# A graph kernel's front: three count tables in turn, zeroed in 16 blocks, with the input read early and its products pipelined

## The reference, cut to what matters

```python
deg = jnp.maximum(segment_sum(ones, dst, 2500), 1.0)
norm = deg ** (-0.5)
h = jnp.maximum(_layernorm(x), 0.0)
hw = norm * (h @ weight)                    # w0 in the kernel
agg = segment_sum(hw[src], dst, 2500)
x = x + relu(agg * norm + bias)
h = jnp.maximum(_layernorm(x), 0.0)
# two layers on h: scores of q[tgt] and k[srcidx] along the edges,
# softmax by target, weighted sum of v, Wo, batch norm, feed-forward
```

## Time and profile before

| | us |
|---|---|
| median of 3 runs | 3387.66 |
| lowest and highest | 3385.79, 3404.86 |
| profiled execution, device time | 3393.12 |
| its span | 3391.3 |
| zeros issued, and landed by the first scatter | 4.1, 73.2 |
| first and last scatter | 73.2, 914.4 |
| last projection of the front ends | 974.0 |

### The profile page before, as it was taken

How to read it: one execution, slowest core, us unless ns; L and a number is a source line. 1 busy time by engine, 2 the same in 40 slices (tenths; PEclk the granted TensorE clock), 3 DMA queues, 4 the chain that set the end, 5 groups by cost and what they waited for, 6 DMA issues and landing times. The chain is left out here.

```text
span 3391.3 us, 72342 instructions
## 1 busy us (share of the span) xinstructions
PE 2990.1 (88%) x24802; PEld 2279.6 (67%) x24802; DVE 2267.0 (67%) x6951; ACT 1965.5 (58%) x3918; POOL 2155.7 (64%) x1991
## 2 busy tenths in 40 slices
PE   2368999978869999999999989989999999999985
PEld 2124655645537778887787877757777778888874
DVE  8594334332337888888888853227888888888856
ACT  0123444433337788888787821227787788888834
POOL 1687877778617777777777710007777777777734
PEclk9999999988989999999999989999999999999998
DMA  9666666645579888888888831238898988888852
GB/s 372 102 126 157 125 122 130 114 91 92 99 194 171 168 166 170 170 175 175 162 167 174 156 84 25 52 72 177 166 166 166 174 171 171 168 173 173 162 120 61
DMA packets 1297462, 496.76 MB, mean 146 GB/s; under 512 B 1237240, under 2 KB 1262865, under 8 KB 1291408
## 3 DMA queue, kind: packets, MB, share of 16 engines
q1 hardware_dynamic: 1156197, 460.22, 63.7%
q0 software_dynamic: 133120, 0.80, 4.2%
q10 hardware_dynamic: 7788, 31.21, 2.8%
HBM read 153.55 MB, written 80.48 MB: 69 GB/s over the span
## 5 line engine op out<-in xcount | busy, mean ns | idle before, releaser
L1255 POOL TENSOR_TENSOR staged<-prob,staged 125x500 f16<-125x500 f32 x960 | 1071.3, 1122 | 166.0 <-ACT staged L1249 87.0
L1483 DVE CUSTOM_DVE_ANT_0 prob<-s_ps,mask 125x500 f32<-125x500 f32 x1600 | 1042.3, 673 | 179.5 <-PE s_ps L1333 116.2
L1420 ACT ACTIVATE prob<-prob,neg_max 125x1000 f32<-125x1000 f32 (+1 forms) x960 | 954.7, 994 | 58.9 <-DVE scrap L1489 53.8
L1333 PE MATMUL s_ps<-keys,queries 128*128 128x500 f16 x3200 | 945.7, 377 | 43.7 <-DMA queries<-q_tiles 28.0
L529 POOL DMA_INDIRECT counts<-count,cell x320 | 653.3, 2042 | 256.3 <-issue 98.1
L1361 PE MATMUL o_ps<-values,across 125*128 125x128 f16 x7680 | 586.8, 219 | 63.9 <-DMA across<-staged 63.4
L1361 PEld LDWEIGHTS o_ps<-values,across 125*128 125x128 f16 x7680 | 502.7, 97 | 200.8 <-issue 70.1
L1249 POOL CAST staged<-prob 125x500 f16<-125x500 f32 x640 | 385.5, 602 | 334.4 <-ACT prob L1420 201.6
L1496 DVE TENSOR_TENSOR p_lo<-t_ps,p_hi 125x500 f16<-125x500 f32 x640 | 434.4, 679 | 171.6 <-ACT p_hi L1430 167.2
L1430 ACT CAST p_hi<-t_ps 125x500 f16<-125x500 f32 x640 | 364.0, 569 | 146.3 <-PE t_ps L1344 145.0
L1344 PEld LDWEIGHTS t_ps<-identity,prob 125*125 125x125 f32 x2560 | 378.2, 188 | 92.0 <-ACT prob L1420 4.4
(11 more groups left out here) (162 smaller groups left out, 3684.2 us busy)
## 6 DMA issues: line engine op xcount, KB each, us to landing
mask<-bias_rows SPq DMA_DIRECT2D x200, 218.8 KB
counts<-xt ACTq DMA_DIRECT2D x8, 3054.0 KB, 37.2
keys<-counts SPq DMA_DIRECT2D x40, 546.9 KB
bias_rows<-edge_bias SPq DMA_DIRECT2D x20, 1093.8 KB
queries<-q_tiles SPq DMA_DIRECT2D x80, 250.0 KB, 3.9
pair_row<-pair_flat SPq DMA_DIRECT2D x40, 437.5 KB
across<-staged SPq DMA_TRANSPOSE x960, 3.0
q_tiles<-q_both SPq DMA_DIRECT2D x80, 125.0 KB, 3.0
```

The costliest lines, as they stand in the source:

```text
L1255: engine.tensor_tensor(here[0:P, BPC:2 * BPC, 0:P], prob[u % PROBS][:, k * KC:(k + 1) * KC].rearrange("p (s c) -> p s c", s=BPC), here[0:P ...
L1333: mm = pe.matmul(s_ps[n % SB][:, 0:KC], lhsT=queries_sb[b][:, at:at + 128], rhs=keys[:, h, c * KC:(c + 1) * KC], start=(part == 0), stop=( ...
L1420: act.activation(here, here, ACT.Exp, bias=neg_max[u % 4][:, :], accum_out=sums[u // H % 2][:, u % H, piece:piece + 1]).then_inc(exped, 1)
L1483: dve.tensor_tensor_reduce(out=prob[u % PROBS][:, at], in0=s_ps[n % SB][0:P, 0:KC], in1=bias[b][:, at], scale=1.0, scalar=MASKED, op0=ALU. ...
```

## The change

- **Three tables.** `counts` becomes three separate tables of N x N cells, and group q writes table q % 3, behind group q - 3. `load_parts` issues six DMAs instead of four, and `merge` adds twice per piece. The three tables together are 37.5 MB.
- **Zeros in 16 blocks.** A block is a sixteenth of each of the three tables, in 3 DMAs of 0.78 MB (runs of 3052 bytes). ACT issues block 0; SP issues block k once all before it have landed, behind the load of pair row k + 1, which itself waits for one of three buffers (`ROWS = 3`). POOL begins once the zeros that `tallies` 0 to 3 can reach are there (`zeros_due`, worked out on DVE); from scatter 32 on it wants all of them.
- **x early**, in two parts right behind block 0 on ACT.
- **w0 products pipelined:** ACT turns tile t + 1 and makes h of t + 2 before it scales tile t, and PE turns t + 1 before it multiplies t.
- **Norm behind ten tally blocks:** one-hots, `tallies` 0 to 2, degrees, statistics of x, `tallies` 3 to 9, then `norm`.
- The last group of each tile is found with small PE transposes and two DVE operations on 20 partitions instead of 20 on 125. `merge(0)` stands ahead of the wait for `hw`, and `first_done` behind it.

```diff
-SIDES = 2
-ROW = SIDES * N
-ZCOLS = 12216
-ZDMAS = 8
+SIDES = 3
+ZCOLS = 3052
 ZREP = 2
+ZDMAS = 16
+GATED = 4
+ROWS = 3
...
+        def zero_block(engine, k):
+            for n in range(SIDES):
+                engine.dma_start(counts[n][k * ZCELLS:(k + 1) * ZCELLS, :].rearrange("(p r c) o -> p r (c o)", p=128, r=ZREP),
+                                 zero_rows).then_inc(zeroed, 16)
...
+                def load_pairs(k):
+                    if k >= ROWS:
+                        sp.wait_ge(rows_used, k - ROWS + 1)
...
+                load_pairs(0)
+                load_pairs(1)
+                for k in range(1, ZDMAS):
+                    load_pairs(k + 1)
+                    sp.wait_ge(zeroed, SIDES * 16 * k)
+                    zero_block(sp, k)
...
+                for k in range(ZDMAS + 1, NB):
+                    load_pairs(k)
...
-                pool.wait_ge(zeroed, 16 * ZDMAS)
                 for q in range(NG):
                     n, turn = q % SIDES, q // SIDES
                     if q % PER_ROW == 0:
-                        pool.wait_ge(cells_ready, q // PER_ROW + 1)
+                        k = q // PER_ROW
+                        pool.wait_ge(cells_ready, k + 1)
+                        if k < GATED:
+                            blocks = pool.value_load(zeros_due_i[0:1, k:k + 1], min_val=SIDES * 16, max_val=SIDES * 16 * ZDMAS)
+                            pool.wait_ge(zeroed, blocks)
+                            apart(pool, waits_met)
+                        elif k == GATED:
+                            pool.wait_ge(zeroed, SIDES * 16 * ZDMAS)
                     if turn > 0:
                         pool.wait_ge(group_writes[n], 16 * GC * turn)
                         pool.sem_inc(groups_landed, 1)
...
                 def merge(t):
...
-                    for k in range(NKC):
-                        dve.tensor_tensor(cnt[b][:, piece(k)], parts[b][:, piece(k)], parts[b][:, N + k * KC:N + (k + 1) * KC],
-                                          ALU.add).then_inc(merged, 1)
+                    for k in range(NKC + 1):
+                        if k < NKC:
+                            steps.done(dve.tensor_tensor(cnt[b][:, piece(k)], parts[b][0][:, piece(k)], parts[b][1][:, piece(k)],
+                                                         ALU.add))
+                        if k > 0:
+                            steps.wait(but=1 if k < NKC else 0)
+                            dve.tensor_tensor(cnt[b][:, piece(k - 1)], cnt[b][:, piece(k - 1)], parts[b][2][:, piece(k - 1)],
+                                              ALU.add).then_inc(merged, 1)
...
+                nodes_h(0)
+                nodes_h(1)
+                turned_h(0)
+                act.wait_ge(deg_loaded, 16)
+                act.activation(deg_root[:, :], deg_col[:, :], ACT.Sqrt).then_inc(roots_ready, 1)
+                act.wait_ge(norm_ready, 1)
+                for t in range(NT):
+                    if t + 1 < NT:
+                        turned_h(t + 1)
+                    if t + 2 < NT:
+                        nodes_h(t + 2)
+                    scaled_hw(t)
```

More of the change, by code:

```diff
@@ L151, in sb @@
         return ctx.enter_context(nc.sbuf_tensor(name, shape, dt))
-    counts = dram("counts", [TABLE, 1], U16)
+    counts = [dram(f"counts{n}", [TABLE, 1], U16) for n in range(SIDES)]
     bias_rows = dram("bias_rows", [N, N], F32)
@@ L539, in tallies @@
                 def tallies(k):
-                    dve.wait_ge(rows_loaded[k % 2], BOTH * (k // 2 + 1))
+                    dve.wait_ge(rows_loaded[k % ROWS], BOTH * (k // ROWS + 1))
+                    here = tally[k % 2]
+                    if k < GATED:
+                        steps.done(dve.tensor_reduce(most[:, :], pair_row[k % ROWS][0:1, :], AXX, ALU.max))
                     for c in range(BC):
@@ L547, in tallies @@
                         steps.done(dve.scalar_tensor_tensor(
[L548 to L549 removed]
+                            matches[c % 2][:, :], pair_row[k % ROWS][:, own], pair[:, at:at + 1],
+                            earlier[:, after:after + GE], ALU.is_equal, ALU.mult, accum_out=here[:, c:c + 1]))
                     steps.wait()
@@ L589, in _ @@
-                for k in range(EARLY):
-                    tallies(k)
-                for half in range(HALVES):
-                    for t in range(TH):
-                        steps.done(dve.scalar_tensor_tensor(below[:, t, :], dst_i[:, :], float(P * (half * TH + t + 1)),
-                                                            group_i[:, :], ALU.is_lt, ALU.mult))
-                    steps.wait()
-                    steps.done(dve.tensor_reduce(needed[:, half * TH:(half + 1) * TH], below[:, :, :], AXX, ALU.max))
-                    steps.wait()
@@ L599, in _ @@
-                dve.sem_inc(needed_ready, 1)
-                for k in range(EARLY, AHEAD):
-                    tallies(k)
-                dve.wait_ge(x_loaded, BOTH)
+                dve.sem_inc(needed_ready, 1)
+                onehots(0)
+                onehots(1)
+                tallies(0)
+                for q in range(2, 5):
+                    onehots(q)
+                tallies(1)
+                for q in range(5, QP):
+                    onehots(q)
+                tallies(2)
+                dve.wait_ge(onehots_used, QP)
@@ L703, in _ @@
                 merge(0)
+                dve.wait_ge(hw_ready, NT)
+                dve.sem_inc(first_done, 1)
+                dve.wait_ge(bias0_loaded, 16)
                 for t in range(APART):
```

266 lines of the change are left out of this document (164 added, 102 removed).

## The result

The changed kernel takes 3398.38 us (median of 19 runs, 3390.02 to 3409.07) beside 3387.19 us for the kernel before (19 runs, 3378.20 to 3404.86): a ratio of 1.003, with a 95% interval of 1.0018 to 1.0042. It is 11 us slower, where 21 us less were forecast. The profiled execution took 3392.59 us (span 3390.8). From the start of the front's last projection to the end of the span 2405 to 2421 us pass in the 13 profiled executions of this study, with the same code. That spread of 16 us is wider than what the front lost, so the front is read from the traces, and the whole from medians and ratios.

A forecast was written before the change was run, and what follows sets the result against it. Scatters were taken to set when PE starts tile 16, and so the front's end. Tile 16 at 774 instead of 800.8 gave -26.8 us, the last tiles +5.7: -21, from the median 3387.7 to 3367, range 3343 to 3416.

The forecast's parts named there:

- Z: The moment at which all zeros have landed: 73 us in the kernel before, forecast at 180.
- Z, before block 5: DVE's one-hots, first tally blocks and statistics of x, until zero block 5 goes out: 82 us.
- one-hots start at about 10 us: Start of DVE's chain to block 5: the first one-hots at about 10 us.
- Z, from block 5 on: Eleven remaining zero blocks at 8.7 us each, 6.2 for zeros and 2.5 for the gap: Z = 180.
- Rival (1): Zeros are slow, short runs costing per packet as x's do (214 GB/s): Z = 236, time 3423; chance 0.12.
- POOL after Z: Scatters 32 to 274 at 2.35 us, 10 us of landing waits: scatter 274 at Z + 579, tile 16 at Z + 594.
- Rival (3): The third table frees no landing waits, as loads and stores fill the DMA engines: tile 16 at 822, time 3415; chance 0.13.
- DVE and PE after Z: Remaining tallies, merge(0), then PE's tiles: tile 0 about Z + 99, tile 16 at Z + 585.
- The w0 products: PE's products without round trips: 4.35 us a tile instead of 6.50, ending at 200, worth nothing at the end.
- The last tiles: Tile 17 is 3.3 us late, tiles 18 and 19 pay 1.2 each: 5.7 us lost in all.
- The sum: Tile 16 at 774 instead of 800.8 (-26.8), plus 5.7 for the last tiles: -21 us, so 3367.
- point of decision, Z = 201: Up to Z = 201, a zero block of 10.6 us, the change gains; beyond it, slow zeros decide.

The follow-up runs named there:

- e11: The changed kernel with zero blocks 6 to 15 issued one behind the other, no pair row between them and no landing wait: ratio 1.0051, 3399.5 us.
- e3: The changed kernel with two tables instead of three: ratio 1.0035, 3396.1 us.
- e10: The changed kernel with zeros streamed, the early merge, each zero block ahead of the pair row, and two tables: ratio 0.9964, 3369.9 us.
- e4: The changed kernel with the w0 products written one tile behind the other again: ratio 1.003, 3392.5 us.
- e1: The changed kernel with zero blocks 5 to 15 not waiting for the landing of the block before: ratio 0.9987, 3382.3 us.
- e7: The changed kernel with the edits of e1 and e6 together: ratio 0.9948, 3361.6 us.
- e6: The changed kernel with the next tile's load ahead of k and v stores and its merge ahead of this tile's low parts: ratio 0.9974, 3373.3 us.
- e5: The changed kernel with all zeros issued by ACT at the start, x behind them, and POOL waiting for all: ratio 1.0059, 3404.6 us.
- e2: The changed kernel with the third table loaded but not added in tiles 17 to 19: ratio 0.9994, 3380.4 us.

## Why the prediction was wrong

**Z, before block 5: 89 instead of 82.** The step "one-hots start at about 10 us" failed: the load of `src_i` lands at 14.9, ten operations follow, and the first one-hot starts at 17.84 (9.34 before).

```profile
14.90 0.49 DVE L644 SCALAR_TENSOR_TENSOR pair<-dst_i,src_i 125x320 f32<-125x320 int32 x1 [8.62 <-DMA src_i<-src_cols]
```

In the kernel before this operation started at 5.79. There ACT began to issue zeros at 4.08, behind a fill of the zero rows of 2.60 us, when SP had issued these loads; the new fill takes 0.69 us, and ACT begins at 1.70, ahead of them. That they queue behind zeros and x is likely from this order, but no run tests it. From there the order held, a 1 x 1000 reduction measured 1.18 us against 1.1 forecast, and the statistics of x came at 70.8 without a wait.

**Z, from block 5 on: 10.5 us a block instead of 8.7.** This is the step on which the forecast broke. "With the issue 2.5 us, and the next pair row (0.5 MB) moves in it" was false. The pair row was priced at nothing; it moves together with the last of the zeros, keeps the engines busy, and only then comes the gap. By the differences between runs it costs 1.9 to 2.6 us a block. The zeros were priced too low as well: 6.2 us at 380 GB/s, where e11 has 343 GB/s and 6.8 to 7.5 us; only the first 1.9 MB of a block go at 390. Against this the gap itself, 0.7 to 1.1 us, was priced too high at 2.5. Seven microseconds at the start and 11 times 1.8 are 27 us, less the 2 allowed for scatters: Z at 204. Rival (1) had a part of the cause, since the zeros move more slowly than 380 GB/s, but at 343 and not at its 214. That 10.5 us a block is just under its deciding 10.6 owes more to the pair row, which it did not name. (Two sums are off besides: 5.7 us of zeros and 2.5 make 8.2 us a block and Z = 174, not 7.9 and 169; and 13.5 us a block gives Z = 232, not 236. The forecast doesn't rest on either.)

The rule cited ahead, of the Trainium skill, "DMA: Bandwidth & Descriptors", section Bandwidth, gave 341 GB/s for DMAs of 1 MB. The 343 GB/s of DMAs of 0.78 MB in e11 agree with it better than the rows from which 380 was taken. But its table is of loads from DRAM, one size at a time, and these are stores in a full queue; a block that goes out alone starts at 390 here.

**POOL after Z: right.** Scatter 274 at Z + 583 (579 forecast), landing waits 16 us (10 forecast). Rival (3) fell, by e3 and e10.

**DVE and PE after Z: a term missing.** Tile 0 came at Z + 100 as forecast. But tiles 0 and 1 took 27.8 and 33.8 us instead of 22.3 and 30.9: the doubled merge makes PE wait for 3.70 us before tile 1 (with two tables, in e3, there is no wait there and the tiles take 22.0 and 30.9), and the matmuls behind it lose more to the clock (5.73 us for eight instead of 3.70; the stretch from 304 to 366 has a mean of 0.89, that from 280 to 334 before had 0.94). So tile 16 came by PE, at Z + 595 and not 585. That this is the 594 forecast for POOL is luck; the same second addition that was priced at 1.2 us a tile at the end was given no price here.

**The w0 products: right in what they are worth**, which is nothing, by e4, and 3.87 us a tile (4.35 forecast). Their end was wrong: `norm` came at 127, not 113, PE then stood for 59 us in front of the last groups, and the products ended at 267, not 200.

**The last tiles: +10 instead of +5.7.** The terms priced were nearly right: PE's wait for the first values grew by 3.2 us before tile 17 (3.3 forecast) and by 1.2 before each of tiles 18 and 19 (1.2 forecast). Two terms were left out. A further 0.48 us is waited for the second piece in tiles 18 and 19. And the matmuls behind the longer pauses begin at half the clock, which costs 1.4, 1.3 and 1.6 us. These make 10.9; against them 0.9 us was gained within tile 16, before which PE no longer waits and whose first matmuls no longer run at half the clock.

**The sum:** tile 16 at -1.9 instead of -26.8, and these 25 us are Z's, since tile 16 came at Z + 595 as forecast (594), if by luck and the other chain; the tail at +10. The said point of decision, Z = 201, was near: Z came at 204, tile 16 gained next to nothing, and the tail decided the sign. The change was 0.3% slower where 0.6% faster was forecast, inside the 1% called "the same".

## What to carry to other kernels

A transfer that shares its queue with another was not hidden in the other's gap here: price it by the engines' busy share while it moves, not by the peak in its slices. Wait for the landing of a block only where something is gained by it; here waiting for the first four blocks and streaming the rest gave 0.3 to 0.4% (e1, and e7 beside e6), while issuing all of them at once held x back and lost 0.3% (e5). And where a steady chain has a short wait, a microsecond of work ahead of it can cost more than itself, since in these traces the clock was at its lower level behind the longer pause; work that can be done a tile earlier should be.

## What the runs showed of the hardware

- Zeros written in runs of 3052 bytes moved 390 GB/s in slices while one block of 2.3 MB was under way at a time, but 343 over 60 us with the queue kept full (e11). The scatters that ran beside it for the first 38 us hardly held it back: from 95 to 125 us it was 340, from 125 to 155, with three scatters, 347.
- The 0.5 MB of a pair row and the last 0.4 MB of a block's zeros, in one queue, kept the DMA engines busy for 4.1 us at some 210 GB/s.
- In the changed kernel, pauses of PE of 3.17 and 0.48 us before tile 19 were followed by eight matmuls in 5.29 us, at a mean granted clock of 0.67 (between 1.2 and 2.4 GHz, the first at the lower one); behind a pause of 1.99 us before, they took 3.67, at 1.00. The two waits and 4.9 to 5.3 us stood so in tiles 18 and 19 of the changed kernel, of e4 and of e11, all with the late double merge. It is the pause that goes with it and not the second addition: tile 17 of e2, with one addition and a pause of 3.51 us, has 5.35 us for the same eight.
